# Expert tiles of a mixture-of-experts kernel: value products moved ahead of the transposes, and filler products taken out of the router

## The reference

```python
def _L0_ffn_ref(x, Wg, W11, W12, W2):          # H=256, I=512, E=8, K=2
    gate_scores = jax.nn.softmax(x @ Wg, axis=-1)
    topk_scores, topk_idx = jax.lax.top_k(gate_scores, K)
    topk_scores = topk_scores / (topk_scores.sum(-1, keepdims=True) + 1e-08)
    gate = jnp.einsum('bsh,ehi->bsei', x, W11)
    value = jnp.einsum('bsh,ehi->bsei', x, W12)
    fused = gate * jax.nn.sigmoid(gate) * value
    expert_out = jnp.einsum('bsei,eih->bseh', fused, W2)
    gathered = jnp.take_along_axis(expert_out, topk_idx[..., None], axis=2)
    return jnp.sum(topk_scores[..., None] * gathered, axis=2)
...
x = x + 0.5 * _L0_ffn_ref(_layernorm(x, axis=-1), ...)
x = x + _L0_attn_ref(_layernorm(x, axis=-1), ...)
x = x + 0.5 * _L0_ffn_ref(_layernorm(x, axis=-1), ...)
```

## Time and profile before

| | us |
|---|---|
| median of 3 runs | 958.73 (958.6 to 959.55) |
| profiled execution, whole | 965.39 |
| its span, first to last instruction | 963.6 |
| mean granted TensorE clock in it | 0.983 of full |
| one-hot products, first pass | from 43.96 to 55.3 |
| tiles, first pass | from 61.1 to 419.4 |
| one-hot products, second pass | from 585.3 to 593.3 |
| tiles, second pass | from 600.0 to the end |

### The profile page before, as it was taken

The page is one execution under the profiler, slowest core; times in us unless marked ns, Lnnn a source line. Parts: engine busy times, 40 slices in busy tenths (PEclk is TensorE's granted clock), DMA queues, the critical chain, the costliest instruction groups (busy, mean ns, idle before and its releaser), DMA issues.

```text
span 963.6 us, 19180 instructions
## 1 busy us (share of the span) xinstructions
PE 904.5 (94%) x5458; PEld 773.9 (80%) x5459; DVE 583.7 (61%) x1386; ACT 389.3 (40%) x768; POOL 575.2 (60%) x616
## 2 busy tenths in 40 slices
PE   7979999999999999958999996999999999999994
PEld 7748888888888888845876873788888888888883
DVE  4876565665656655558836997555555555555551
ACT  3834343343343433315634775233333333333331
POOL 4845655665655666417604653477777777777762
PEclk9989999999999999989999998999999999999998
DMA  9743616436254373149202556744433434333331
GB/s 322 259 145 124 209 57 205 164 98 202 66 190 157 106 241 124 39 157 300 90 0 88 173 161 216 246 103 79 80 54 71 79 52 77 54 76 54 54 45 23
DMA packets 83745, 121.51 MB, mean 126 GB/s; under 512 B 12944, under 2 KB 62480, under 8 KB 83696
## 3 DMA queue, kind: packets, MB, share of 16 engines
q0 software_dynamic: 25088, 37.59, 17.8%
q1 hardware_dynamic: 43504, 56.05, 17.7%
q10 hardware_dynamic: 15104, 27.28, 8.5%
HBM read 73.62 MB, written 47.25 MB: 125 GB/s over the span
## 4 chain that ended last, share of the span: by engine, by line
PE 81%; DVE 6%; issue 4%; DMA 3%; ACT 2%; POOL 1%; another core or an unknown queue 1%; ACTq 1%; POOLq 0%; SPq 0%; DVEq 0%
PE bank L1501 37%; PE bank L1524 19%; PE bank L1510 6%; PE bank L1623 3%; PE bank L1684 3%; PE bank L1493 3%; PE bank L1436 3%; PE bank L1674 1%; PE bank L1703 1%; PE bank L1640 1%; DMA w_lo<-w_lo_rows 1%; DMA out_rows<-yb,idx_i 1%; PE bank L1611 1%; PE bank L1694 1%
## 5 line engine op out<-in xcount | busy, mean ns | idle before, releaser
L1204 DVE TENSOR_TENSOR sg<-sg,bank 128x512 f32<-128x512 f32 x142 | 97.6, 687 | 283.3 <-ACT sg L758 188.0
L1501 PE MATMUL bank<-w_hi,xt_hi 128*128 x568 | 237.3, 418 | 7.7 <-DVE xt_lo L1193 4.2
L1501 PE MATMUL bank<-w_hi,xt_lo 128*128 x568 | 224.1, 394 | 0.0
L1501 PE MATMUL bank<-w_lo,xt_hi 128*128 x568 | 223.9, 394 | 0.0
L750 ACT ACTIVATE yb<-bank,gates_in 128x256 f32<-128x256 f32 x142 | 67.3, 474 | 315.9 <-PE bank L1524 252.5
L554 POOL DMA_INDIRECT xg<-xn_rows,idx_i x142 | 139.9, 985 | 61.6 <-issue 42.0
L558 POOL DMA_INDIRECT gates_in<-gate_rows,idx_g x142 | 135.8, 957 | 53.7 <-issue 42.7
L1524 PE MATMUL bank<-w_hi,ft_hi 128*128 x568 | 160.1, 282 | 2.2 <-ACT yb L750 2.2
L1524 PE MATMUL bank<-w_lo,ft_hi 128*128 x568 | 160.3, 282 | 0.0
L1524 PE MATMUL bank<-w_hi,ft_lo 128*128 x568 | 160.2, 282 | 0.0
L568 POOL DMA_INDIRECT out_rows<-yb,idx_i x71 | 114.7, 1616 | 59.0 <-ACT yb L750 27.5
(11 more groups left out here) (290 smaller groups left out, 1297.8 us busy)
## 6 DMA issues: line engine op xcount, KB each, us to landing
w_lo<-w_lo_rows SPq DMA_DIRECT2D x32, 512.0 KB
w_lo_rows<-w_lo ACTq DMA_DIRECT2D x16, 512.0 KB
xn_rows<-work SPq DMA_DIRECT2D x13, 512.0 KB, 3.2
x_all<-x SPq DMA_DIRECT2D x8, 512.0 KB, 10.3
w_lo_rows<-in_sb ACTq DMA_DIRECT2D x16, 256.0 KB
gate<-x SPq DMA_DIRECT2D x16, 256.0 KB, 7.8
seq<-y_rows SPq DMA_DIRECT2D x8, 512.0 KB, 5.2
seq<-w ACTq DMA_DIRECT2D x7, 512.0 KB
```

The lines of the kernel that those rows point to most:

```text
L1204: nc.vector.tensor_tensor(sg[p], sg[p], ps_g[p][:], ALU.mult).then_inc(f_step, 1)
L1501: last = nc.tensor.matmul(dst[p][:], xt[p][:, c, :], of(w), start=(c == 0 and n == 0), stop=(c == DC - 1 and n == len(parts) - 1))
```

## The change

In a tile, PE makes the value products directly behind the gate products; the 2 and the 4 transposes come behind both, ahead of `down`. In the router, the filler products between the groups of one-hot products are gone (17 in the first pass, 8 in the second). The fillers behind the groups stay. DVE, ACT, POOL and SP have the same instructions in the same order.

```diff
@@ router(r)
                 for n in range(NQB):
-                    if n >= 2:
-                        idle = ((10, 7), (8, 0))[r][n - 2]
-                        keep_busy(ps_g[0][:], before.unsqueeze(1).to_broadcast([P, G, P]), idle)
                     pe.wait_ge(first_step, r * NQB + n + 1)
@@ experts(r), tile(t, h, q)
                     up(p, w11_hi, w11_lo, ps_g, e, g_done)
+                    up(p, w12_hi, w12_lo, ps_v, e, v_done)
                     if early != ET - 1:
                         rows_in(h + (q + 1) // XG, (q + 1) % XG)
                     if early > 0:
                         hidden_in(t - 1, 1 - p)
-                    up(p, w12_hi, w12_lo, ps_v, e, v_done)
                     if early > 1:
                         down(t - 2, p, e_before)
```

## The result

The changed kernel takes 962.08 us (median of 11 runs), the kernel before, run beside it, 959.41: a ratio of 1.0025, 95% interval 1.0015 to 1.0035. That is slower by 2.4 us, 1.4 to 3.4. The forecast was 1.2 us.

The account below looks back on a forecast made before the run. PE, busy for 94% of the span, was taken to set the pace of both passes. The terms 0 - 0.4 + 0.3 + 0.4 + 0.9 = +1.2 on the median 958.73 gave 959.9 us, range 956.5 to 965.

Parts of the forecast that it names:

- half-clock case: Second pass's first tile: clock still at half, +2.4; with +0.6 for first tiles +4.2 in all, 962.9; chance 0.33.
- The tile, steady: Each steady tile on PE: same 30 instructions, still 4.84 us, `xt_lo` cover shrinking from 1.16 to 0.72; price 0.
- The rival that it is late in each tile: Steady tiles: `xt_lo` late if its cover is below 0.72; 0.1 per tile gives +14, 973; chance 0.05.
- The cheaper `down`: Steady tiles: first weights of `down` loaded beneath the transposes, making each tile faster; -11, 948; chance 0.03.
- Waits in mid first pass: First pass's middle tiles: hidden transposes' waits for `fu` go because PE has value products to do; -0.4, bounds -1.0 and 0.
- Router, first pass, and first tiles: First pass's start: fourth group at half clock, +0.6, tiles 0 and 1 +0.8, mostly absorbed by ACT's wait; +0.3.
- Last tile, first pass: End of first pass: `fu` comes later, last hidden transposes start later, the next `down` starts 0.4 later; +0.4.
- Router, second pass: Second pass's one-hot products: without fillers most of the third and fourth groups run at half clock, DVE waits; +0.9.
- First tiles of the second pass: Tiles 0 and 1, second pass: later `xt_lo` costs +0.8, taken as lost in a wait; 0, bounds 0 and +0.8.

Follow-up runs that it names:

- rows_last: Kernel before with value products ahead of the transposes in every tile and the next rows' two transposes behind the four hidden ones, fillers kept: 964.66 us, ratio 1.0035.
- Order_first_mid: Kernel before with value products ahead of the transposes only in tiles 2 to 69 of the first pass, all fillers kept: 960.30 us, ratio 0.9994.
- order_mid: Kernel before with value products ahead of the transposes only in tiles 2 to 69 of each pass, all fillers kept: 968.67 us, ratio 1.0019.
- fillers_first: Kernel before without the 17 fillers of the first pass's router, the 8 of the second and the old order kept: 966.33 us, ratio 1.0003.
- loads_early: Changed kernel with PE loading the last two `down` expert numbers ahead of the last hidden transposes: 971.62 us, ratio 1.0066 to the kernel before.
- fillers_second: Kernel before without the 8 fillers of the second pass's router, the 17 of the first and the old order kept: 967.37 us, ratio 1.0011.
- after_again: The changed kernel again, with no further edit, beside the kernel before on another chip: 971.35 us against 966.69, ratio 1.0059.
- order_ends: Kernel before with value products ahead of the transposes only in tiles 0, 1 and 70 of both passes, all fillers kept: 962.69 us, ratio 1.0025.
- order_second_pass: Kernel before with value products ahead of the transposes only in the second pass's tiles, all fillers kept: 961.46 us, ratio 1.0011.

## Why the prediction was right, and where not

The measured 962.08 lies in the prediction's range of 956.5 to 965, and the forecast has the right direction. Its size is half of what was measured, 1.2 against 2.4. That the number lies inside owes something to luck: it is above the forecast's own range (957.5 to 961.5) and near the 962.9 of the half-clock case, which is why the range reached so far, and that case did not happen in the changed kernel's profiles. Term by term:

- **The tile, steady: 0.** Right, 4.85, in the main comparison and in every profile with the new order. The cover of `xt_lo` was read as 0.72 and measured as 805.35 - 804.57 = 0.78. The rival that it is late in each tile fell with rows_last. The cheaper `down` fell too: `down` now pays for the load behind the transposes (302 ns).
- **Waits in mid first pass: -0.4.** Not shown. Order_first_mid is -0.6 with an interval from -1.4 to +0.3, so on a quiet chip the term may be there. On another chip order_mid, with both passes' middles, was +1.8. The waits for `fu` did go, as the term says. Where ACT and DVE stop often, PE waited ahead of the gate products instead, and its idle in all was larger than before.
- **Router, first pass, and first tiles: +0.3.** The mechanism was right: half clock for the fourth group, DVE hiding a part (+0.65 is left, +0.6 was forecast), full clock in the first tile in return. The size isn't resolved. Fillers_first gives +0.3 for the router's part, with an interval from -1.1 to +1.6; the traces have the first `down` of the pass 0.3 to 0.7 earlier than before.
- **Last tile, first pass: +0.4.** Wrong in size, measured 1.02. The chain to `fu` was right (the wait of 0.68 came), but the sentence that the next `down` starts 0.44 behind the transposes left out what is queued on PE behind the waiting instruction: the load of an expert number. loads_early took 0.64 of the 1.02 back, and the 0.38 that stayed is the forecast's +0.4.
- **Router, second pass: +0.9.** Right within what the runs show: +0.7 to +0.8 in four traces, +1.2 in the one of the main comparison, and +1.0 (0.1 to 1.9) by fillers_second. Half clock was the cause, as read, though it took both groups in two profiles (in one of them the fourth in part) and only the fourth in three. By the page of the Trainium skill named in the prediction ("TensorE: Matmul & The Clock Gate", "Why this matters for your kernels") gaps between bursts take the clock to half. The trace agrees in the first pass: 3.63 of idle, and then 2.05 for a group that had taken 1.23 behind 1.26 of idle. It isn't that simple in the second pass: in the changed kernel's profile the clock was at half before the idle of 1.87, and in after_again the third group ran at full clock behind 1.48 of idle.
- **First tiles of the second pass: 0, "lost in the wait for the first gates".** Wrong: 0.64 by the tiles' starts, and 0.6 of it still there at the first `down`. In both profiles of before tile 3 is 0.6 to 1.0 longer than 4.85, with PE idle in it (0.44 ahead of the next gate product, 0.74 ahead of the hidden transposes). The changed kernel's first profile has no such stop (tile 3 takes 4.85). Neither have order_first_mid and order_ends, which differ by 0.6 there, so nothing swallows the delay where the stop is missing.
- **The half-clock rival.** The first tile of the second pass ran at full clock in the changed kernel's profile. Over all fourteen profiles it ran below full in five, three of them with all fillers of that router and the old or the new order (order_mid, order_second_pass, rows_last), one with them and none in the first router (fillers_first), one without any (loads_early). So it is a matter of the run and not what the change does. To the first `down` it costs 0.3 to 2.0 us: 12.05 and 12.98 against 11.75 in the old order, 13.87 and 14.28 against 12.3 in the new.

The sum with the measured terms is 0.9 to 1.0 (last tile) + 0.6 (first tiles of the second pass) + 0.7 to 1.2 (second router), and for the first router and tiles something from -0.7 (traces) to +0.3 (fillers_first): 1.5 to 3.1, which the measured 1.4 to 3.4 holds. The two mis-sized terms, the last tile of the first pass and the first tiles of the second, were each 0.6 too small, and that alone would make up the difference to 2.4.

The extra 2 to 3 us that the order costs on two of the chips stay open. Theory C (shorter idle stretches at DVE and ACT hide less of their stops) fits that the long intervals moved, that PE's idle in mid pass is about 1.3 larger on average where the stops are many, and that there is no such cost where the stops are few. But rows_last, which should have made more of them, ran on the quiet chip, and the sums of the long intervals differ by less than two profiles of one kernel do. It was not shown.

No version beat the kernel before clearly. The nearest is order_first_mid, and its interval includes 1.

## What to carry to other kernels

Moving work inside a loop that the busiest engine fills cost nothing in its steady turns here, since each hand-over kept its cover (0.35 us was still enough). The price stood in the first and last turns, where the work that gave the cover is missing, so look there. When a wait is added to an in-order queue, list what stands behind it, register loads and address arithmetic too: here they started only when the wait ended. Filler products earned their place where another engine waits for the group behind them (the second router, +1.0); in the first router the sums came 0.65 later as well, and no loss was measured beyond the spread of the runs.

## What the runs showed that was not expected

- On TensorE the load of an expert number, with its arithmetic, behind a semaphore wait cost 0.4 of visible idle and 0.64 in the distance of the `down` of tiles 68 and 69.
- With the fillers between the groups of the first router taken out, the first tile behind it ran at full clock in five profiles of five, with them in four of nine. Chance alone would deal it out like that about once in sixteen, so it is a hint.
- The same kernel took 966.5 us on two chips and 959 to 961 on two others, and the cost of one edit differed between them by more than its interval (1.0025, 1.0015 to 1.0035, and 1.0059, 1.0042 to 1.0076). A ratio from one chip is a ratio for that chip.
